# Expert stage: who weighs the hidden products, VectorE or GpSimd

## The reference

```python
q = (x_norm @ wq).reshape(B, T, HEADS, 2, DIM_KEY)      # HEADS 8, DIM_KEY 32
sim = jnp.einsum('bthpd,hkpd->pbthk', q, keys)          # 64 keys in each half
s1, i1 = jax.lax.top_k(sim[0], K)                       # K 16
s2, i2 = jax.lax.top_k(sim[1], K)
all_idx = (i1[..., :, None] * NUM_KEYS + i2[..., None, :]).reshape(B, T, HEADS, K * K)
all_scores = (s1[..., :, None] + s2[..., None, :]).reshape(B, T, HEADS, K * K)
final_scores, pk = jax.lax.top_k(all_scores, K)
final_idx = jnp.take_along_axis(all_idx, pk, axis=-1)
wd = expert_down[final_idx]
wu = expert_up[final_idx]
hidden = jax.nn.gelu(jnp.einsum('btd,bthkd->bthk', x_norm, wd), approximate=False)
hidden = hidden * jax.nn.relu(final_scores)
out = jnp.einsum('bthk,bthkd->btd', hidden, wu)
```

## Time and profile before

| | us |
|---|---|
| median of 3 runs | 2791.85 (2786.22 to 2799.73) |
| the profiled execution | 2792.13, its span 2790.4 |
| TensorE busy | 2273.1 (81%) |
| weight loads | 1972.7 (71%) |
| VectorE busy | 1860.9 (67%) |
| ScalarE busy | 663.8 (24%) |
| GpSimd busy | 433.8 (16%) |

### The profile page before, as it was taken

How to read it: one execution, slowest core, us unless ns; L and a number is a source line. 1 busy time by engine, 2 the same in 40 slices (tenths; PEclk the granted TensorE clock), 3 DMA queues, 4 the chain that set the end, 5 groups by cost and what they waited for, 6 DMA issues and landing times. The chain is left out here.

```text
span 2790.4 us, 50156 instructions
## 1 busy us (share of the span) xinstructions
PE 2273.1 (81%) x18017; PEld 1972.7 (71%) x18017; DVE 1860.9 (67%) x7732; ACT 663.8 (24%) x1527; POOL 433.8 (16%) x521
## 2 busy tenths in 40 slices
PE   6676888874889889889989989989887788747994
PEld 3455777753789889889888888889887566425663
DVE  4335555536898898898898898899893656550002
ACT  2442444433211211211211211211211334401220
POOL 2013333320011011011101101101103200030003
PEclk8787899977777887887787787787786788868996
DMA  1104333305100000000000000000000322042423
GB/s 51 33 29 110 83 80 84 71 13 145 31 1 5 5 1 5 5 1 5 5 4 2 5 4 2 5 4 2 1 1 7 79 60 64 12 153 66 125 89 98
DMA packets 87043, 107.85 MB, mean 39 GB/s; under 512 B 26222, under 2 KB 75502, under 8 KB 86062
## 3 DMA queue, kind: packets, MB, share of 16 engines
q1 hardware_dynamic: 81328, 96.62, 13.3%
q0 software_dynamic: 3296, 6.43, 0.9%
q10 hardware_dynamic: 2176, 1.61, 0.2%
HBM read 70.61 MB, written 30.51 MB: 36 GB/s over the span
## 5 line engine op out<-in xcount | busy, mean ns | idle before, releaser
L1539 PE MATMUL peer_x_ps<-peer_oh_h,peer_oh_a 128*128 128x32 bf16 x3136 | 417.3, 249 | 6.1 <-DVE peer_oh_l L1811 4.4
L1539 PEld LDWEIGHTS peer_x_ps<-peer_oh_h,peer_oh_a 128*128 128x128 bf16 x3136 | 414.0, 149 | 8.8 <-DVE peer_oh_l L1811 5.8
L1540 PE MATMUL peer_x_ps<-peer_oh_l,peer_oh_a 128*128 128x32 bf16 x3136 | 417.9, 249 | 0.0
L1540 PEld LDWEIGHTS peer_x_ps<-peer_oh_l,peer_oh_a 128*128 128x128 bf16 x3136 | 412.7, 149 | 3.5 <-issue 1.4
L1549 PE MATMUL peer_out_ps<-peer_g,peer_up 128*128 128x224 f32 x1792 | 373.9, 375 | 30.6 <-issue 28.4
L1515 PE MATMUL peer_x_ps<-peer_xc,peer_dt 128*128 128x224 f32 x1792 | 371.9, 371 | 31.8 <-DMA peer_up<-in_L_ffn_expert_up_dram 19.7
L1549 PEld LDWEIGHTS peer_out_ps<-peer_g,peer_up 128*128 128x128 f32 x1792 | 363.5, 205 | 38.2 <-issue 32.4
L1515 PEld LDWEIGHTS peer_x_ps<-peer_xc,peer_dt 128*128 128x128 f32 x1792 | 360.3, 203 | 39.6 <-issue 34.6
L1481 POOL TENSOR_TENSOR peer_g<-peer_g,peer_qt 128x448 f32<-128x448 f32 x112 | 189.0, 1708 | 1279.5 <-ACT peer_qt L1638 1279.0
L1276 DVE TENSOR_REDUCE l_attn_mx<-l_attn_s_ps 98x4 f32<-98x392 f32 (+1 forms) x320 | 178.3, 563 | 236.8 <-PE l_attn_s_ps L1046 154.8
L1616 ACT ACTIVATE peer_g<-peer_x_ps 128x448 f32<-128x448 f32 x224 | 121.7, 543 | 651.4 <-PE peer_x_ps L1515 651.4
(11 more groups left out here) (308 smaller groups left out, 3713.4 us busy)
## 6 DMA issues: line engine op xcount, KB each, us to landing
moe_w<-in_L_ffn_w_dram SPq DMA_DIRECT2D x16, 1024.0 KB, 9.0
l_attn_pieces_q_dram<-l_attn_pieces_q SPq DMA_DIRECT2D x16, 294.0 KB, 3.1
l_attn_pieces_k_dram<-l_attn_pieces_k SPq DMA_DIRECT2D x16, 294.0 KB, 2.9
l_attn_stq<-l_attn_pieces_q_dram SPq DMA_DIRECT2D x16, 294.0 KB
l_attn_stk<-l_attn_pieces_k_dram SPq DMA_DIRECT2D x16, 294.0 KB
peer_g<-n_L_ffn_expert_down_dram SPq DMA_DIRECT2D x8, 512.0 KB, 6.7
peer_up<-in_L_ffn_expert_up_dram SPq DMA_DIRECT2D x2, 2048.0 KB
l_xi<-net_x SPq DMA_DIRECT2D x16, 196.0 KB, 2.3
```

The costliest lines, as they stand in the source:

```text
L1539: nc.tensor.matmul(x_ps[q][:, i * J:(i + 1) * J], oh_a[hb % 2][:, :, t], oh_h[hb % 2][:, :, t], start=True, stop=False)
L1540: mm = nc.tensor.matmul(x_ps[q][:, i * J:(i + 1) * J], oh_a[hb % 2][:, :, t], oh_l[hb % 2][:, :, t], start=False, stop=True)
```

## The change

`weigh` is gone. In all four half tiles ScalarE copies each quarter from PSUM to SBUF and GpSimd multiplies the copy into `g`; its multiply now raises `g_done`. The two copy buffers are a tensor of their own (`m_both`) instead of `qt`, so ScalarE's score copies may come between them. `t1`, `t2`, `t3` of `make_codes` lie in `m_both`, so that VectorE waits there for `g_done` of the whole chunk (it was `m_done`). TensorE's scatter of half tiles 1 to 3, and the first four hidden pairs of the next chunk, wait for `m_copied`.

```diff
@@ chunk of gpsimd
-                for hb in range(LATE, NHB):
+                for hb in range(NHB):
                     for q in range(4):
-                        pool.wait_ge(m_copied, 4 * (NHB - LATE) * n + 4 * (hb - LATE) + q + 1)
+                        pool.wait_ge(m_copied, 4 * NHB * n + 4 * hb + q + 1)
                         ts = slice(hb * HT + q * GT, hb * HT + (q + 1) * GT)
                         nc.gpsimd.tensor_tensor(g[:, :, ts], g[:, :, ts], m_copy[q % 2].rearrange("p (t j) -> p j t", j=J),
-                                                ALU.mult).then_inc(g_done_late, 1)
+                                                ALU.mult).then_inc(g_done, 1)
@@ scatter of tensor
-                    elif hb < LATE + 1:
-                        pe.wait_ge(g_done, 4 * LATE * n + 4 * (hb - 1) + q + 1)
                     else:
-                        pe.wait_ge(m_copied, 4 * (NHB - LATE) * n + 4 * (hb - 1 - LATE) + q + 1)
+                        pe.wait_ge(m_copied, 4 * NHB * n + 4 * (hb - 1) + q + 1)
@@ chunk of scalar
-                    for t in range(NTILE):
-                        score_out(n + 1, t)
-                for k in range(4 * (NHB - LATE)):
-                    act.wait_ge(m_done, 4 * NHB * n + 4 * LATE + k + 1)
-                    wait(act, g_done_late, 4 * (NHB - LATE) * n + k - 1)
-                    nc.scalar.activation(m_copy[k % 2], x_ps[k % 4][:, 0:GT * J], ACT.Copy).then_inc(m_copied, 1)
+                for hb in range(NHB):
+                    for q in range(4):
+                        k = 4 * hb + q
+                        act.wait_ge(m_done, 4 * NHB * n + k + 1)
+                        wait(act, g_done, 4 * NHB * n + k - 1)
+                        nc.scalar.activation(m_copy[k % 2], x_ps[q][:, 0:GT * J], ACT.Copy).then_inc(m_copied, 1)
+                    if hb < NTILE and not last:
+                        score_out(n + 1, hb)
@@ make_codes of vector
-                wait(dve, m_done, 4 * NHB * n)
+                wait(dve, g_done, 4 * NHB * n)
@@ chunk of vector
                 for hb in range(NHB - 1):
                     one_hots(n, hb + 1)
-                    if hb < LATE:
-                        weigh(n, hb)
```

More of the change, by code:

```diff
@@ L1370, in peer_ffn @@
     NHB = 2 * NTILE
-    LATE = NHB // 2
     GT = HT // 4
@@ L1389, in peer_ffn @@
         qt = S.sb("qt", [P, 4, CT])
-        m_copy = [qt[:, 2 * p:2 * p + 2, :].rearrange("p m t -> p (m t)") for p in range(2)]
+        m_both = S.sb("m_both", [P, 2, GT * J])
+        m_copy = [m_both[:, p, :] for p in range(2)]
         sc = [S.sb(f"sc{p}", [TT, G16, NK]) for p in range(NTILE)]
@@ L1398, in peer_ffn @@
         pos_b, col_b = S.sb("pos_b", [TT, PP], BF16), S.sb("col_b", [TT, PP], BF16)
-        t1, t2, t3 = S.sb("t1", [TT, PP]), S.sb("t2", [TT, PP]), S.sb("t3", [TT, PP])
+        t1, t2, t3 = (m_both[0:TT, :, :].rearrange("p c n -> p (c n)")[:, i * PP:(i + 1) * PP] for i in range(3))
         bits, col = S.sb("bits", [TT, PP], U32), S.sb("col", [TT, PP], U32)
@@ L1509, in hidden @@
                     if jp < 4:
-                        wait(pe, m_copied, 4 * (NHB - LATE) * n - 3 + jp)
+                        wait(pe, m_copied, 4 * NHB * n - 3 + jp)
                     else:
@@ L1543, in experts_out @@
             def experts_out(n):
-                pe.wait_ge(g_done, 4 * LATE * (n + 1))
-                pe.wait_ge(g_done_late, 4 * (NHB - LATE) * (n + 1))
+                pe.wait_ge(g_done, 4 * NHB * (n + 1))
                 wait(pe, x_done, n)
@@ L1701, in fold @@
                 else:
-                    chain.step(nc.vector.tensor_tensor(out[:, :], m[:, 0, :], m[:, 1, :], ALU.add))
+                    chain.step(nc.vector.tensor_tensor(out, m[:, 0, :], m[:, 1, :], ALU.add))
             def top_halves(n, t):
@@ L1759, in make_codes @@
                 chain.wait(but=1)
-                chain.step(nc.vector.scalar_tensor_tensor(bits[:, :], t1[:, :], 15.0, t3[:, :], ALU.add, ALU.add))
+                chain.step(nc.vector.scalar_tensor_tensor(bits[:, :], t1, 15.0, t3, ALU.add, ALU.add))
                 chain.wait(but=1)
@@ L1780, in make_codes @@
                 chain.wait()
-                chain.step(nc.vector.tensor_scalar(t1[:, :], i2[:, :], 32.0, 64.0, ALU.is_ge, ALU.mult))
+                chain.step(nc.vector.tensor_scalar(t1, i2, 32.0, 64.0, ALU.is_ge, ALU.mult))
                 chain.wait()
                 row, column = (codes[:, c, :].rearrange("t (h k) -> t k h", k=TOP) for c in range(2))
-                nc.vector.tensor_tensor(row, by_rank(t1[:, :]), by_rank(i1[:, :]), ALU.add)
-                nc.vector.scalar_tensor_tensor(column, by_rank(t1[:, :]), -0.5, by_rank(i2[:, :]), ALU.mult, ALU.add).then_inc(codes_ready, 1)
+                nc.vector.tensor_tensor(row, by_rank(t1), by_rank(i1), ALU.add)
+                nc.vector.scalar_tensor_tensor(column, by_rank(t1), -0.5, by_rank(i2), ALU.mult, ALU.add).then_inc(codes_ready, 1)
             def low_weights(n, t):
@@ L1812, in one_hots @@
                 ins.then_inc(oh_ready, 1)
[L1814 to L1820, removed]
             for t in range(NTILE):
```

10 lines of the change are left out of this document (5 added, 5 removed).

## The result

The changed kernel is slower. Its median is 2835.19 us (2826.80 to 2844.41, 4 runs), against 2789.74 (2786.22 to 2799.73, 4 runs) for the kernel before on the same chip: a ratio of 1.0158, 95% interval 1.0114 to 1.0202, or 45 us. The forecast was 2835. Across the chips used for the experiments the median of the kernel before lies between 2789.7 and 2800.7 us, so those are compared by their ratio to it (the 95% interval stands in brackets behind each), and by their traces.

What follows compares the result with a forecast made beforehand. The bound was taken as a ring through scatter 1's end, VectorE's one-hots 3, searches and codes, and TensorE's turn. Terms -3.9, +44.6 and +2.5 give +43.2 us on 2792.1, 2835 us; range 2806 to 2862.

Steps and rivals of the forecast that it cites:

- The weighs lie in waiting time: VectorE, expert stage: only 0.53 us of weighs per chunk change lies on the ring, 6.9 us at most over 13.
- the replay: Chunk 4 stepped through with the change: one-hots 2 ends at 18.5, one-hots 3 at 30.5 against 27.1.
- Turns: VectorE one-hots and GpSimd multiplies alternate by whole instructions, 1.24 us a block; 52 blocks in one-hots 3 instead of 16.
- The chunk changes: The 13 chunk changes: start 0.3 us earlier, -3.9 us; 36 more blocks of 1.24 us, +44.6 us.
- the last chunk: Last chunk, where scatter 3 waits for the one-hots: -2.6 for weighs, +3.7 + 0.2 and +1.24 for blocks, +2.5 us.
- Nothing from the added waits: ScalarE's 112 added copies, the two-buffer ring and the codes' wait for all 16 multiplies cost nothing.
- The turn's clock: TensorE from codes' turn to next scatter: clock change kept at zero; +8 if slower, -18 if fast everywhere.
- rival 2: Blocked time feeds back: late one-hots 2 delays one-hots 3, slow clock every turn; +27 us, 2862 us; chance 0.10.
- Rival 1: Blocks do not multiply: GpSimd's multiplies drain before one-hots 3, weighs gone, 2783 us; chance 0.13.
- Rival 3: Searches come 2 us or more earlier and TensorE's chain takes over; at most 77.6 us go, 2714 us; chance 0.04.
- Rival 4: Only short one-hots L1808 and L1811 blocked, two more per chunk; +28, 2820 us; chance 0.73 together with the forecast.
- the ring: Steps setting the chunk period: scatter start, scatter 1's end, one-hots 3, searches and codes, turn, hidden products, queries, next scatter.

Runs made afterwards that it cites:

- tiny_multiply: Changed kernel with every GpSimd multiply cut to one element per partition, all waits and copies kept; ratio 0.9899 to the kernel before.
- before_held: As own_buffer, and GpSimd's first multiply of half tile 2 waits until the one-hots of half tile 3 are written; ratio 0.9922 to the kernel before.
- own_buffer: Changed kernel with VectorE weighing half tiles 0 and 1 again; copy buffer, codes' wait and ScalarE's order stay; ratio 1.0009 to the kernel before.
- no_input: Changed kernel with GpSimd's multiply replaced by a fill of 1.0 that reads nothing, behind a one-element multiply; ratio 0.9945 to the kernel before.
- one_input: Changed kernel with GpSimd's multiply replaced by the copy times 1.0, behind a one-element multiply; ratio 0.9910 to the kernel before.

## Why the prediction was right

The sum was 43.2 us, measured were 45 by the medians. That forecast and median agree to 0.2 us is luck: the sum was put on a run 2.4 us above the median of the kernel before, the changed kernel's four runs lie 17.6 us apart, and its trace holds 5.9 us between turn and scatter that the sum had at zero. The mechanism is not luck, and the traces bear it out step by step:

- **The weighs lie in waiting time.** Predicted gain 0.53 us per chunk, from the earlier start of one-hots 3. It starts at 18.45 instead of 18.66 on average, so 0.2 was gained: one-hots 2 ends at 18.5 and took the rest, as the replay had it (0.3). With the blocks away on both sides, the weighs are worth 0.44 us: the first search comes at 25.23 in `tiny_multiply` and at 25.67 in `before_held`.
- **Turns.** One block predicted at 1.24 us; the four in one-hots 3 of chunk 4 are 1.18, 1.31, 1.18 and 1.27 us. Number of blocks: three in one-hots 2 and four in one-hots 3, as predicted, the 128-row instruction among them, which no row of before had shown blocked. One-hots 3 ends at 30.35 (30.5 predicted), scatter 3 starts at 30.41 (30.6), the last multiply ends at 40.0 (40), the period is 106.99 (106 to 107).
- **The chunk changes** cost 39.7 us up to the first search (40.7 predicted), **the last chunk** 2.35 (2.5).
- **Nothing from the added waits**: `own_buffer` bears it out for the codes' wait and the buffer, within its interval, and `tiny_multiply` for the copies.
- **The turn's clock** was kept at zero. The traces differ by 5.9 us there, 5 us of which `own_buffer` shows as well; no run tells the rest of the change from the scatter of executions. The length does not simply grow with the wait ahead of it: in the changed kernel's trace four turns after 3.5 to 5.7 us of waiting take 17.7 to 17.8 us to the next scatter, five after 8.1 to 8.2 us take 16.3 to 16.4. Why is open.
- **Sizes that were off:** the multiplies' mean (1.9 predicted, 2.20), because two long ones in each chunk were not in it: the fourth, 4.76 us, and the one that waits under the first instruction of one-hots 3, 5.16 us. And that one-hots 2 has no slack left did not feed back as rival 2 feared: it ends at 18.5, 0.3 us behind the scatter (18.2), and one-hots 3 follows at once.
- **A reading that was loose:** the prediction gives the searches one tensor input. The rows name two for FIND_INDEX8 (`peer_i<-peer_v,peer_sc`), and it keeps its 0.22 us beside the multiplies all the same.

Rival 1 (no multiplied blocks) fell with the seven stretched instructions in each chunk. Rival 3 (VectorE is soon not the bound) did not arise: the searches came later, not earlier. Rival 4 (half effect) fell with the 128-row instruction, which is blocked in one-hots 3 of every chunk.

The rule of the Trainium skill, "SBUF — State Buffer" (Who interferes with whom), that a VectorE instruction with two SBUF inputs contends with a GpSimd one that reads SBUF, and not with one that only writes it, agrees with these traces: the one-hots go from 1.09 to 2.4 us beside the multiplies, and keep 1.09 beside the fills of `no_input`. The same section of the Trainium skill says that the other engine fully blocks while the first has the ports for its whole instruction. The one-element multiply does wait to the end of VectorE's instruction (3.32 us). But VectorE loses less than GpSimd's instruction lasts: 1.2 to 1.3 of 1.36 us beside the multiply, and only 0.75 of 1.71 us beside the one-tensor product.

## What to carry to other kernels

An engine's busy or waiting total says what could be freed, the ring says what is worth freeing: 163 us of weighing and waiting on VectorE had some 10 us on the ring, by the prediction's sum. Moving element-wise work from VectorE to GpSimd was not free here, where GpSimd reads SBUF beside VectorE instructions that read two SBUF tensors. Count the VectorE instructions on the ring that will meet it, and take at most one GpSimd instruction's length for each. Then place the GpSimd work beside VectorE instructions that keep their length (here the searches), with a wait if need be. If the engine that looks slack waits ahead of a point on the ring, move its work from behind that point to ahead of it.

## What the runs showed of the hardware

- Where VectorE's one-hots and GpSimd's multiplies, both reading two SBUF tensors, stand one behind the other in their lists, they take turns by whole instructions: each VectorE instruction of 1.09 or 3.88 us loses 1.18 to 1.31 us (chunk 4), and cutting the long one in two adds one such loss.
- A one-element GpSimd multiply of two SBUF tensors takes 0.19 us alone and 3.32 us when asked for under a VectorE instruction of 3.9 us with two SBUF tensors.
- VectorE's searches (MAX8, FIND_INDEX8, MATCH_REPLACE8) keep their length beside GpSimd's multiplies in the changed kernel (0.21 to 0.22 us with or without one), and a GpSimd fill of 128 x 448 keeps 0.49 us beside VectorE's one-hots.
- GpSimd's product of one tensor with a constant takes 1.71 us, longer than the product of two tensors of the same size (1.36), and holds VectorE up by 0.75 us at a time.
- After 8.24 us without work TensorE's stretch from turn to scatter took 16.3 us at a mean granted clock of 0.82 (changed kernel, chunk 4); the same work after 0.88 us took 14.1 us at 1.00 (`one_input`, chunk 4).
